# A two-layer block on one core: the routing's products move to another PSUM bank and half a body later, and the steps behind the attention are spread over all positions

## What is computed

```
x = x + LN(attn(LN(x)));   x = x + LN(ffn(LN(x)))
attn: x = x + token_diffusion(LN(x)*w1+b1) * gamma1      # 16 heads of 16, a softmax over 512 x 512 for each head
      x = x + channel_diffusion(LN(x)*w2+b2) * gamma2    # 8 heads of 32 channels, a softmax over 32 x 32
ffn:  probs = softmax(x @ w_router)                      # 8 experts, the best two of each token
      out = sum over its two experts of weight * (gelu(x @ w1[e] + b1[e]) @ w2[e] + b2[e])
```

## Time and profile before

| what | us |
|---|---|
| median of 3 runs (1291.8 to 1295.47) | 1293.74 |
| the profiled execution | 1295.4 |
| its span, first to last instruction | 1293.6 |
| PE busy in the span, with weight loads apart | 1041.8 (81%) |
| ACT, DVE, POOL busy | 711.8, 671.5, 395.3 |
| PE waiting in `prefix` for DVE (L1045 <- DVE L790), whole span | 40.9 |
| PE waiting in `mix` for DVE (L1002 <- DVE L733), whole span | 20.2 |

### The profile page before, as it was taken

One profiled execution on the slowest core, in us unless ns is written; L12 is line 12 of the kernel. 1 busy time (PEld: TensorE's weight loads), 2 busy tenths in 40 slices (PEclk: granted clock), 3 DMA queues, 4 the chain that ended last, 5 costly groups with the idle time before them and its releaser, 6 DMA issues. The chain is left out here.

```text
span 1293.6 us, 17851 instructions
## 1 busy us (share of the span) xinstructions
PE 1041.8 (81%) x6108; PEld 732.2 (57%) x6108; DVE 671.5 (52%) x1824; ACT 711.8 (55%) x1077; POOL 395.3 (31%) x342
## 2 busy tenths in 40 slices
PE   4598979879799788898854249999999999989900
PEld 1223544435444354444443139999899899989900
DVE  5124455354553645333333536566665665668748
ACT  1486566645666455665500046675665766767713
POOL 5002023040230402212120342345354453434332
PEclk9698899889898898989957569999999999999955
DMA  6652634626346263464040062434234243356263
GB/s 233 102 101 50 184 65 95 183 61 185 67 97 177 58 184 71 101 171 166 1 165 1 33 257 81 157 118 182 110 133 175 112 171 128 113 177 226 94 245 152
DMA packets 44769, 167.51 MB, mean 129 GB/s; under 512 B 9392, under 2 KB 15920, under 8 KB 35504
## 3 DMA queue, kind: packets, MB, share of 16 engines
q1 hardware_dynamic: 32580, 131.53, 34.1%
q0 software_dynamic: 10560, 29.14, 6.6%
q10 hardware_dynamic: 1548, 5.82, 1.6%
HBM read 102.75 MB, written 63.70 MB: 129 GB/s over the span
## 5 line engine op out<-in xcount | busy, mean ns | idle before, releaser
L536 ACT ACTIVATE E<-PS,VV 128x1024 f32<-128x1024 f32 x256 | 270.2, 1118 | 114.4 <-PE PS L865 114.4
L1437 PE MATMUL PY<-W2P,HP 128*128 128x256 f32 x1872 | 231.6, 285 | 2.2 <-DVE Y L1332 2.2
L1437 PEld LDWEIGHTS PY<-W2P,HP 128*128 128x128 f32 x1872 | 227.4, 193 | 2.4 <-DVE Y L1332 2.4
L1409 PE MATMUL PH<-XP,W1P 128*128 128x512 f32 (+1 forms) x1104 | 221.4, 360 | 3.7 <-DVE W1P L1363 3.7
L1409 PEld LDWEIGHTS PH<-XP,W1P 128*128 128x128 f32 x1104 | 185.9, 191 | 33.8 <-issue 4.0
L1375 DVE TENSOR_TENSOR HP<-PH,HP 128x512 fp32r<-128x512 f32 x156 | 107.9, 691 | 86.1 <-ACT HP L1313 85.8
L1258 POOL DMA_INDIRECT choice_rows<-Y,DI x78 | 76.1, 976 | 247.6 <-DVE Y L1332 230.9
L865 PE MATMUL PS<-OPB,OPA 102*128 102x512 bf16 x512 | 139.9, 389 | 13.9 <-DMA OPB<-norm_parts 7.8
L848 PE MATMUL PO<-E,VA 128*32 128x512 f32 x1024 | 144.8, 637 | 0.4 <-ACT E L536 0.4
L865 PEld LDWEIGHTS PS<-OPB,OPA 102*128 102x128 bf16 x512 | 37.8, 99 | 165.3 <-issue 69.2
L1308 ACT ACTIVATE PH<-PH,B 128x512 f32<-128x512 f32 (+1 forms) x184 | 107.4, 596 | 27.0 <-PE PH L1409 18.8
(11 more groups left out here) (202 smaller groups left out, 1326.0 us busy)
## 6 DMA issues: line engine op xcount, KB each, us to landing
expert_rows<-ZERO SPq DMA_DIRECT2D x8, 4160.0 KB, 17.8
WG<-experts SPq DMA_DIRECT2D x23, 1152.0 KB, 5.2
WG<-experts SPq DMA_DIRECT2D x23, 1028.0 KB, 6.9
OPB<-q_parts SPq DMA_DIRECT2D x84, 128.0 KB
YC<-choice_rows SPq DMA_DIRECT2D x8, 1024.0 KB, 8.2
q_parts<-QP SPq DMA_DIRECT2D x128, 48.0 KB
OPA<-q_parts SPq DMA_DIRECT2D x16, 384.0 KB
X<-x SPq DMA_DIRECT2D x8, 512.0 KB, 10.9
```

The costliest lines, as they stand in the source:

```text
L536: a.activation(E[:, s % 2, h, :, :], PS[:, u % 2, :, :], ACT.Exp, scale=vec("tau_t")[:, 4 * (s // 2) + h:4 * (s // 2) + h + 1]).then_inc(e ...
L1409: last = m.matmul(PH[:, u % BANKS, at:at + w], W1P[:, a, k * HID + c * P:k * HID + c * P + P], XP[:, o, k, 0:w], start=(k == 0 and (a, o) ...
L1437: last = m.matmul(PY[:, i, :], HP[:, a, at:at + P], W2P[:, o, c * D:(c + 1) * D], start=(c == 0 and (a, o) == terms[0] and i % 2 == 0), st ...
```

## The change

The late steps no longer share `PB` with the post steps. They write to `PA`, between the pre steps `sq` (position 7) and `v0` (position 14): four uses for a batch, each waiting for the reading of the one before (`give_late`), with semaphores and a chain of their own. They move from positions 1 to 3 to positions 8 to 13 of the same body. The exponential of the routing and DVE's work behind it become a step of their own, `soft`, at position 10. Of the post steps, `x2t`, `qkc`, `gram`, `clear` and `dist` go one position later; ACT's exponential of the channel diffusion becomes a step `soft_c` one position behind `dist`; `mix` goes from 11 to 13, `weff` from 11 to 14 and `chan` from 12 to 15. `Z3T` now lies in the buffer of `QF` instead of `OTN`, so ACT waits for the readers of `QF` before it writes `Z3T`, and `qk0` and `qk1` for the reader of `Z3T`. No instruction on data is added or removed.

```diff
-PRE_USES, POST_USES = 7, 22
+PRE_USES, POST_USES, LATE_USES = 7, 18, 4
+BEHIND = 3
...
-POST_AT = {2: ['residual'], 3: ['untok0'], 4: ['untok1', 'ontok'], 5: ['proj'], 7: ['x2t'], 8: ['qkc'], 9: ['gram', 'clear'], 10: ['dist'], 11: ['mix', 'weff'], 12: ['chan']}
-LATE_AT = {1: ['z3t'], 2: ['logits'], 3: ['prefix']}
+POST_AT = {2: ['residual'], 3: ['untok0'], 4: ['untok1', 'ontok'], 5: ['proj'], 8: ['x2t'], 9: ['qkc'], 10: ['gram', 'clear'],
+           11: ['dist'], 12: ['soft_c'], 13: ['mix'], 14: ['weff'], 15: ['chan']}
+LATE_AT = {8: ['z3t'], 9: ['logits'], 10: ['soft'], 13: ['prefix']}
...
-            Z2, X2T, QC, Z3T = ON, OTN, ON, OTN
+            Z2, X2T, QC, Z3T = ON, OTN, ON, QF
...
+            late_full, late_free, late_links = sem("late_full"), sem("late_free"), sem("late_links")
...
+            def late_over(b):
+
+                return LATE_USES * (b + 1)
...
+                        at_least(act, lg_ready, b - BEHIND + 1)
...
                 def z3t(b, par):
+                    if not isinstance(b, int) or b + BEHIND < B:
+                        act.wait_ge(sq_ready, KC * (b + BEHIND + 1))
+                        act.wait_ge(qp_ready, KC * (b + BEHIND + 1))
                     for k in range(KC):
-                        a.copy(Z3T[:, k, :], takep(b, 18 + k)).then_inc(post_free[k], 1)
+                        act.wait_ge(late_full, LATE_USES * b + k + 1)
+                        a.copy(Z3T[:, k, :], PA[:, :]).then_inc(late_free, 1)
                 do["z3t"] = z3t
...
-                def dist(b, par):
+                def soft_c(b, par):
                     act.wait_ge(l_ready, b + 1)
                     for k in range(2):
                         a.activation(LX[:, k, :], L[:, k, :], ACT.Exp, bias=LS[:, 1, k:k + 1],
                                      accum_out=LS[:, 2, k:k + 1]).then_inc(lx_ready, 1)
-                do["dist"] = dist
-
-                def logits(b, par):
-                    act.wait_ge(lg_ready, b + 1)
+                do["soft_c"] = soft_c
+
+                def soft(b, par):
+                    act.wait_ge(lg_ready, b + 2)
                     a.activation(PR[:, :, :], LG[:, :, :], ACT.Exp).then_inc(pr_ready, 1)
-                do["logits"] = logits
+                do["soft"] = soft
                 schedule(act, do)
...
+                dve.sem_inc(lg_ready, 1)
...
-                post = Chain(dve, post_links, 3 * STATS + 5 * C + 25)
+                post = Chain(dve, post_links, 3 * STATS + 2 * C + 10)
+                late = Chain(dve, late_links, 3 * C + 15)
...
-                    post.b = b
-                    ps = takep(b, 20)[:, 0:C * NE].rearrange("p (c e) -> p c e", e=NE)
-                    post.did(v.reduce_max(R4[:, 0, :], ps, AX.X))
-                    post.wait()
-                    v.tensor_tensor(LG[:, :, :], ps, bc(R4[:, 0, :]), ALU.subtract).then_inc(post_free[0], 1)
-                    emptied(dve, b, 20)
+                    late.at(b)
+                    dve.wait_ge(late_full, LATE_USES * b + 3)
+                    ps = PA[:, 0:C * NE].rearrange("p (c e) -> p c e", e=NE)
+                    late.did(v.reduce_max(R4[:, 0, :], ps, AX.X))
+                    late.wait()
+                    v.tensor_tensor(LG[:, :, :], ps, bc(R4[:, 0, :]), ALU.subtract).then_inc(late_free, 1)
+                    dve.wait_ge(late_free, LATE_USES * b + 3)
                     v.tensor_copy(PAY[:, :, D + 3], const("token").rearrange("p (b c) -> p b c", c=C)[:, ds(b, 1), :]
                                   .rearrange("p a c -> p (a c)")).then_inc(lg_ready, 1)
+                do["logits"] = logits
+
+                def soft(b, par):
                     dve.wait_ge(pr_ready, b + 1)
-                    post.did(v.reduce_sum(R4[:, 1, :], PR[:, :, :], AX.X))
-                    post.wait()
-                    post.did(v.reciprocal(R4[:, 2, :], R4[:, 1, :]))
-                    post.wait()
-                    post.did(v.tensor_tensor(PR[:, :, :], PR[:, :, :], bc(R4[:, 2, :]), ALU.mult))
-                    post.wait(alone)
+                    late.did(v.reduce_sum(R4[:, 1, :], PR[:, :, :], AX.X))
+                    late.wait()
+                    late.did(v.reciprocal(R4[:, 2, :], R4[:, 1, :]))
+                    late.wait()
+                    late.did(v.tensor_tensor(PR[:, :, :], PR[:, :, :], bc(R4[:, 2, :]), ALU.mult))
+                    late.wait(alone)
...
-                    v.tensor_copy(PX[:, :, :, :], takep(b, 21)[:, 0:2 * C * NE].rearrange("p (k c e) -> p k c e", k=2, c=C)
-                                  ).then_inc(post_free[1], 1)
-                    emptied(dve, b, 21)
+                    dve.wait_ge(late_full, LATE_USES * b + 4)
+                    v.tensor_copy(PX[:, :, :, :], PA[:, 0:2 * C * NE].rearrange("p (k c e) -> p k c e", k=2, c=C)
+                                  ).then_inc(late_free, 1)
+                    dve.wait_ge(late_free, LATE_USES * b + 4)
...
+                    if j == 5:
+                        at_least(pe, late_free, late_over(b - BEHIND))
                     return bank(b, j)
+
+                def give_late(b, j):
+
+                    if j == 0:
+                        if isinstance(b, int) and b + BEHIND >= B:
+                            pe.wait_ge(pre_free, PRE_USES * B)
+                        else:
+                            pe.wait_ge(pre_free, PRE_USES * (b + BEHIND) + 5)
+                    at_least(pe, late_free, LATE_USES * b + j)
+                    return PA
 
                 def givep(b, j):
...
                 def z3t(b, par):
                     pe.wait_ge(z3_ready, b + 1)
                     for k in range(KC):
-                        ps = givep(b, 18 + k)
+                        ps = give_late(b, k)
                         for c in range(C):
                             i = t.transpose(ps[:, c * P:c * P + P], PAY[:, c, k * P:k * P + P], ident)
-                        i.then_inc(post_full, 1)
+                        i.then_inc(late_full, 1)
                 do["z3t"] = z3t
 
                 def logits(b, par):
-                    emptied(pe, b, 18)
-                    emptied(pe, b, 19)
-                    ps = givep(b, 20)
+                    pe.wait_ge(late_free, LATE_USES * b + KC)
+                    ps = give_late(b, 2)
                     for c in range(C):
                         for k in range(KC):
                             i = t.matmul(ps[:, c * NE:c * NE + NE], Z3T[:, k, c * P:c * P + P], vec("router")[:, k * NE:k * NE + NE],
                                          start=(k == 0), stop=(k == KC - 1))
-                    i.then_inc(post_full, 1)
+                    i.then_inc(late_full, 1)
                 do["logits"] = logits
 
                 def prefix(b, par):
                     pe.wait_ge(oh_ready, b + 1)
-                    ps = givep(b, 21)
+                    ps = give_late(b, 3)
                     sel = OH[:, 2, :, :].rearrange("p c e -> p (c e)")
                     t.matmul(ps[:, 0:C * NE], const("lower"), sel, start=True, stop=True)
-                    t.matmul(ps[:, C * NE:2 * C * NE], const("ones"), sel, start=True, stop=True).then_inc(post_full, 1)
+                    t.matmul(ps[:, C * NE:2 * C * NE], const("ones"), sel, start=True, stop=True).then_inc(late_full, 1)
                 do["prefix"] = prefix
                 schedule(pe, do)
```

More of the change, by code:

```diff
@@ L776, in logits @@
                     for c in range(C):
-                        post.did(v.max(TOP[:, c, :], PR[:, c, :]))
-                    post.wait(alone)
+                        late.did(v.max(TOP[:, c, :], PR[:, c, :]))
+                    late.wait(alone)
                     for c in range(C):
[L780 to L783, removed]
+                        late.did(v.max_index(TI[:, c, :], TOP[:, c, :], PR[:, c, :]))
@@ L784, in logits @@
+                    late.wait()
+                    late.did(v.tensor_copy(TF[:, :, 0:2], TI[:, :, 0:2]))
+                    late.wait()
                     iota = const("iota8").rearrange("p (c e) -> p c e", e=NE)
                     for k in range(2):
-                        post.did(v.tensor_tensor(OH[:, k, :, :], iota, bc(TF[:, :, k]), ALU.is_equal))
-                    post.did(v.tensor_copy(PAY[:, :, D:D + 2], TOP[:, :, 0:2]))
-                    post.did(v.tensor_copy(PAY[:, :, D + 2], TF[:, :, 0]))
@@ L789, in logits @@
-                    post.wait()
+                        late.did(v.tensor_tensor(OH[:, k, :, :], iota, bc(TF[:, :, k]), ALU.is_equal))
+                    late.did(v.tensor_copy(PAY[:, :, D:D + 2], TOP[:, :, 0:2]))
+                    late.did(v.tensor_copy(PAY[:, :, D + 2], TF[:, :, 0]))
+                    late.wait()
                     v.tensor_tensor(OH[:, 2, :, :], OH[:, 0, :, :], OH[:, 1, :, :], ALU.add).then_inc(oh_ready, 1)
-                do["logits"] = logits
+                do["soft"] = soft
@@ L798, in prefix @@
+                    dve.wait_ge(late_free, LATE_USES * b + 4)
```

(16 more changed lines are left out.)

## The result

| | kernel before | changed kernel |
|---|---|---|
| median, us | 1294.61 (1291.8 to 1295.74, 4 runs) | 1325.02 (1322.18 to 1325.81, 4 runs) |
| profiled execution, span, us | 1293.6 | 1322.7 |
| mean granted clock | 0.895 | 0.889 |

The ratio is 1.0234 (95% interval 1.0211 to 1.0258), 30 us more. Forecast were 1330 and a range of 1308 to 1348.

The account below looks back on a forecast made before the run. PE's own order of work in stage 1 was taken as the bound. The terms gave +6.7 us in each of five full bodies, +33.5, and +36.5 with the ends: 1330 us, own range 1322 to 1339, 8-in-10 range 1308 to 1348.

Parts of the forecast that it names:

- (a): Positions 2 to 4, which `prefix` leaves: `OH` wait goes, `untok1`'s hidden wait comes out; -1.2 us a body.
- (b): Position 8, `z3t` in one bank: PE's second half waits for ACT's copy of the first; +2.0 us a body.
- (c): Position 11: `dist` waits because DVE does `soft` ahead of `gram`; +2.2 us a body.
- (d): Position 13: `mix` waits behind DVE's `prefix`; +0.9 us, plus 0.3 for a longer low clock, +1.2 a body.
- (e): PE's low clock behind the new waits: 1.5 for (c), 1.0 for (b), together +2.5 us a body, bounds 0 to 4.
- The ends: Outside bodies 2 to 6: body 7 +4 us, body 1 -2, the drain +1.
- Costed at nothing: Operand loads behind the later `clear`, and POOL's powers for `chan` queued behind the scatter, were taken to delay nothing.
- Rival 1: The clock holds: all waits as forecast but (e) is 0; 1316 us, chance 0.22.
- rival 4: Another wait restores the body's length, or gains and losses cancel; 1294 us, chance 0.07.
- rival 2: Every wait lowers the clock, or the scatter is late: (e) 4, (a) -0.2; 1345 us, chance 0.16.
- Rival 3: DVE/POOL collision at `residual` ends, `untok1`'s wait and low clock go: (a) -7.8; 1282 us, chance 0.08.

Follow-up runs that it names:

- e6: Changed kernel with post steps ahead of late steps everywhere, `z3t`'s halves at positions 8 and 9, `logits` and `soft` at 10: ratio 0.9878 to the kernel before.
- e1: Changed kernel with the post step `gram` (`dist`'s chain) ahead of `soft` at position 10 on every engine: ratio 1.0109 to the kernel before.
- e2: Changed kernel with `mix` ahead of `prefix` at position 13 on every engine: ratio 1.0071 to the kernel before.
- e3: Changed kernel with POOL's `residual` waiting until DVE has done its six operations of `qk0` and `qk1`: ratio 1.0002 to the kernel before.
- e8: Kernel before the change with `residual` at position 0 instead of 2: ratio 0.9867 to the kernel before.
- e7: e6 plus e3's wait of POOL's `residual` on DVE: ratio 0.9647 to the kernel before (1248 us on 1294).
- e10: e7 with DVE reading `untok0` ahead of `qk1`'s operations and PE doing `prefix` ahead of `mix`: ratio 0.953 to the kernel before.
- e12: e10 with the loop over bodies 2 to 5 written out: ratio 0.9442 to the kernel before.
- e4: Kernel before the change with POOL's `residual` waiting until DVE has done its six key/query operations: ratio 1.0025 to the kernel before.
- e5: Changed kernel with both order swaps, those of e1 and e2 together: ratio 0.9948 to the kernel before.
- e9: Changed kernel with 12 extra matmuls filling PE's wait ahead of `mix`, from the second batch on: ratio 1.0191 to the kernel before.

## Why the prediction was right, step by step

The waits came where the forecast put them, at nearly its sizes, and the median of 1325 lies in its own range. It was 5 us too high. That the sum is so near is luck in part: the clock cost less than forecast, and (a) gained next to nothing, and these two errors mostly cancel. By its steps, us per full body:

- **(a) -1.2: measured about -0.1.** `qk0` to `proj` took 21.05, 21.82, 23.47, 20.93 and 21.82 in bodies 2 to 6, mean 21.8, where 21.2 was forecast. The 21.9 that I set against it is body 3's, the longest: in the kernel before, bodies 2 to 6 take 24.03, 24.65, 23.80, 24.50 and 23.64, mean 24.1, so 21.4 without the late steps' matmuls. That is +0.4, less the 0.45 of `prefix`. `untok1` waits 5.1 to 5.3, a little over the 4 to 5 forecast. `PAY` takes 2.09 instead of the 1.38 of the earlier trace rows, beside POOL's `SQ` (that POOL is the cause is read from the two timelines; no run removed it alone). And `untok1`'s wait in body 4 is 1.7 longer for the jump, 0.3 a body, which no step had. What I had called hidden until now came out in full.
- **(b) +2.0: 1.81 to 1.87** in each body; e6 shows it as real time.
- **(c) +2.2: 1.83 to 2.10**; e1 shows that DVE's order makes it.
- **(d) +1.2: waits +0.9**, as forecast (3.90 on the mean instead of 2.34 + 0.68); `weff` waits no more; e2 shows DVE's order again. The 0.3 for the clock is in (e).
- **(e) +2.5, with (d)'s 0.3 +2.8: 1.0 is what the other steps leave of 5.6.** This is the term that was mis-sized most. The 1.0 that I gave to (b) was wrong: behind its 1.81 the clock never fell in the changed kernel. Behind (c) it fell in three bodies of five, behind (d) in all. The 2.2 of e1 and e2 is no measure of the same thing: it also holds the low clock that the kernel before already had behind `mix`.
- **The ends.** Body 1 gained 3.4 us, forecast 2. Body 7 (68.2 before, 69.4 after, up to the end of its attention) lost 1.2, forecast 4. The drain lost 3.5, forecast 1. Body 1 had begun 0.7 earlier, which no step explains. Together +0.6, forecast +3.
- **Costed at nothing:** POOL's scatter was over (328.96) 10 us before POOL's first power was wanted (339.33), and PE shows no wait for operands. Both held.

So five bodies gave 28.2 instead of 33.5 and the ends 0.6 instead of 3; the rest of the program is 0.3 later (29.1 in all by the two spans).

Rival 1 (the clock holds) is refuted by the rows of 1.97 and 2.07, rival 4 by the ratio. Of rival 2, (e) stayed far from its 4 and the scatter wasn't late; (a) did come near its -0.2, for the other reasons above. Rival 3 (the collision ends by itself) didn't come: DVE's first two operations started ahead of POOL's product (261.45 and 262.49) and the third was caught nonetheless. Only in body 4 did the six operations take 3.7 us (354.30 to 357.96), because DVE came so late behind the jump that POOL's products were over (353.28), and there it gained nothing. The Trainium skill (SBUF — State Buffer, "Who interferes with whom") states an exclusive lock; the 2.31 and 2.38 us operations beside products of 1.89 and 2.22 agree with it, since each ends only behind a product. DVE got its short operations only where POOL's products did not lie beside them (e3, e8). But rival 3's price was right. It put the six operations at 3.6 us and the gain at 6.6 a body; e3, which made it true by a wait, has 3.7 and gains 30 us with five bodies that could gain.

## What to carry to other kernels

When a wait is moved off a queue, look at what the same queue waits for next: here 31.3 us for `OH` became 27.4 for `ON`, and the gain had to come from the cause behind `ON`, two engines that stretch each other's operations, not from the place of the waiter. Where two chains stand in one engine's order, the one whose reader comes first goes first; two such swaps were worth 37 us, more than the whole change had cost. And here the loop's jump back was hidden as long as DVE had slack at the lap's start (9.60 us); a chain moved to the last position laid it open. Last, a term measured in one body is not the mean: taken over all five, (a) would have been forecast half a microsecond a body less favourable.

## What the runs showed of the hardware

- DVE stands for 5.6 to 8.0 us behind the loop's jump back when it arrives late, with no releaser, in the changed kernel and the eight built on it that keep the loop (in e7 with POOL idle); with the loop written out the gap is gone (e10 and e12).
- POOL's products stretch even DVE's smallest operations: a copy of 8 elements a partition took 1.75 instead of 0.17 us (e4). In these runs a DVE chain of tiny steps was no safer beside POOL than one of large ones.
- The clock behind a wait isn't set by that wait alone. Waits of 1.43 to 1.51 had it at full speed behind them in the matmuls of `mix` in all bodies of e2 and e5, but in e5 the attention products right behind ran at 1.94 in bodies 2, 4 and 6 and at 1.06 in 3 and 5, behind the same 1.51; in e5 the same bodies 2 and 4 ran slow behind `z3t`'s 1.82 (L1001 at 1.92 instead of 1.04). In e6 the same wait of 1.43 in body 1, and 1.51 in body 5, had `mix` itself at 2.07 and 1.93 behind it. In body 7 of the changed kernel a wait of 3.74 had `mix` at 1.13, and the low clock came only with the attention products behind (1.93). In e9, where one wait was filled, low stretches came more often behind another one.
